# Turning every fourth tile of attention counts on TensorE instead of in a DMA transpose, with one DMA transpose per tile for the others

## The reference

```python
q = _fq_sym(q, axis=-1); k = _fq_sym(k, axis=-1); v = _fq_sym(v, axis=2)   # symmetric, 127 steps
attn = jnp.einsum('bhqd,bhkd->bhqk', q, k)
attn = softmax(attn)
attn = _fq_unsigned(attn, axis=-1)        # round(attn / (max/255)), 0..255
out = jnp.einsum('bhqk,bhkd->bhqd', attn, v)
```

## Time and profile before

| | |
|---|---|
| median of 3 runs | 1628.33 us |
| the profiled execution | 1632.03 us, its span 1630.3 us |
| PE, DVE, ACT, POOL busy | 84%, 62%, 46%, 26% of the span |
| mean granted clock of PE | 0.888 |
| first read of scores (L1816) to the end of the last | 1085.8 to 1452.5 us |

### The profile page before, as it was taken

One profiled execution on the slowest core, in us unless ns is written; L12 is line 12 of the kernel. 1 busy time (PEld: TensorE's weight loads), 2 busy tenths in 40 slices (PEclk: granted clock), 3 DMA queues, 4 the chain that ended last, 5 costly groups with the idle time before them and its releaser, 6 DMA issues.

```text
span 1630.3 us, 22435 instructions
## 1 busy us (share of the span) xinstructions
PE 1365.1 (84%) x7972; PEld 660.5 (41%) x7972; DVE 1017.6 (62%) x1722; ACT 756.4 (46%) x1094; POOL 428.8 (26%) x316
## 2 busy tenths in 40 slices
PE   7993989898857999999999999786677676659778
PEld 3441555555524444444444444322222222224334
DVE  5998899999965101111011110898889898864995
ACT  4774788888830111111111111327677776752553
POOL 1114100000004757999940002201111111100341
PEclk9996999999968999999999999877666766769989
DMA  7998565555348999999997996389999999993001
GB/s 252 290 278 165 106 130 117 131 115 115 63 155 304 356 373 368 368 402 395 408 359 294 316 367 225 81 186 212 208 213 212 206 210 210 205 186 78 1 1 52
DMA packets 516726, 355.12 MB, mean 218 GB/s; under 512 B 430856, under 2 KB 432904, under 8 KB 516016
## 3 DMA queue, kind: packets, MB, share of 16 engines
q1 hardware_dynamic: 502896, 308.08, 71.3%
q0 software_dynamic: 9920, 37.75, 6.6%
q10 hardware_dynamic: 3840, 8.39, 1.4%
HBM read 205.86 MB, written 38.01 MB: 150 GB/s over the span
## 4 chain that ended last, share of the span: by engine, by line
PE 48%; DMA 22%; DVE 17%; issue 8%; ACT 3%; POOL 1%; POOLq 0%; SPq 0%; ACTq 0%; DVEq 0%
DMA arena<-arena 20%; PE scores L1021 18%; PE bank L1039 9%; PE bank L904 4%; PE scores L887 2%; DVE arena L1601 2%; PE scores L888 2%; DVE arena L1587 2%; PE scores L1171 2%; ACT arena L1302 2%; PE bank L1207 1%; PE scores L1031 1%; PE scores L1092 1%; DVE arena L1816 1%; POOL arena L779 1%
## 5 line engine op out<-in xcount | busy, mean ns | idle before, releaser
L1816 DVE TENSOR_SCALAR_CACHE_REDUCE arena<-scores,arena 128x1024 f32<-128x1024 f32 x256 | 311.7, 1279 | 36.1 <-PE scores L1092 35.8
L1021 PE MATMUL scores<-arena 128*128 128x512 f32 x736 | 321.4, 595 | 3.3 <-DVE arena L1735 3.3
L1394 ACT ACTIVATE arena<-arena 128x2048 int16<-128x2048 f32 x128 | 255.8, 1999 | 129.2 <-DMA arena<-arena 98.0
L1743 DVE TENSOR_TENSOR arena<-scores,arena 128x512 f32<-128x512 f32 x46 | 31.8, 692 | 446.9 <-PE scores L1021 446.9
L1092 PE MATMUL scores<-arena 96*128 96x512 bf16 x512 | 205.9, 544 | 32.9 <-DVE arena L1816 27.9
L1021 PEld LDWEIGHTS scores<-arena 128*128 128x128 f32 x736 | 140.3, 191 | 180.2 <-issue 176.7
L1039 PE MATMUL bank<-arena 128*128 128x512 f32 x368 | 163.3, 597 | 3.6 <-issue 3.4
L1106 PE MATMUL bank<-arena 128*128 128x32 bf16 x2048 | 64.4, 183 | 94.0 <-DMA arena<-arena 93.9
L1587 DVE TENSOR_REDUCE arena<-scores 128x1 f32<-128x640 f32 (+3 forms) x128 | 127.8, 1019 | 8.5 <-PE scores L865 8.1
L1302 ACT ACTIVATE arena<-scores 128x512 f32<-128x512 f32 (+3 forms) x256 | 116.9, 507 | 25.9 <-PE scores L888 25.8
L1601 DVE TENSOR_TENSOR arena<-arena 128x1024 f16<-128x1024 f32 (+2 forms) x128 | 126.2, 1026 | 3.5 <-issue 1.8
(11 more groups left out here) (277 smaller groups left out, 2041.3 us busy)
## 6 DMA issues: line engine op xcount, KB each, us to landing
arena<-in_L_ffn_w SPq DMA_DIRECT2D x69, 2048.0 KB, 12.8
arena<-arena SPq DMA_DIRECT2D x32, 256.0 KB, 3.0
kst_d<-arena POOLq DMA_DIRECT2D x16, 384.0 KB, 6.6
tern_d<-arena POOLq DMA_DIRECT2D x12, 512.0 KB, 7.0
arena<-kst_d SPq DMA_DIRECT2D x16, 384.0 KB, 4.2
xs_d<-arena SPq DMA_DIRECT2D x23, 256.0 KB, 3.5
arena<-xs_d SPq DMA_DIRECT2D x22, 256.0 KB, 14.0
ys_d<-arena ACTq DMA_DIRECT2D x22, 256.0 KB, 6.7
```

The costliest lines, as they stand in the source:

```text
L1021: ins = pe.matmul(scores[:, m * 1024 + half * 512:m * 1024 + half * 512 + 512], xsT[a][:, c], wa[:, m, c, half * 512:half * 512 + 512], st ...
L1394: act.activation(p16[j % PAIRS_P][:, n % 2], ssb[n % SBUFS], ACT.Exp, bias=ebias[n % SBUFS], scale=-1.0, accum_out=rsum[h % 2][:, t:t + 1] ...
L1816: dve.tensor_scalar(ssb[i][:, d:d + 1024], scores[:, s:s + 1024], nsq[:, h, t:t + 1], None, ALU.mult, ALU.min, accum_out=nmx[i][:, half:ha ...
```

## The change

- `p16` and `pT` are used as 6 and 4 single tiles (`PBUFS`, `TBUFS`), in the same memory as the pairs.
- Three tiles of four (n % 4 = 0, 1, 2) are turned by a DMA transpose each, of 128 x 2048 counts (512 KiB). It waits for `av_done` of the tile four before.
- Tiles with n % 4 = 3 (`by_pe`) are turned on PE: the counts are taken as 1024 words of 32 bits, and 8 transposes of 128 x 128 words go into banks 4 and 5 (`a1_turn`, three tiles behind the scores). ACT copies both banks into `pT` (`copy_turned`, two copies of 128 x 512 words, behind the exponential of tile n + 2).
- A word holds two counts, so ACT writes the counts of such a tile in an interleaved order (four-dimensional patterns for `dst` and `src`), and the products read `pT` with a step of two elements between columns.
- Banks 4 and 5 are no longer free for scores: these go round two slots instead of three, half m in slot m % 2, and PE waits for the read of the half two before.
- The products stand five tiles behind the scores, one tile at a time, those of a turned tile six behind.
- Semaphores are shared to make room (`q0_in` with `x_loaded`, `wdT_in` with `wT_in`); what waits for them waits for correspondingly higher counts.

```diff
-PAIRS_P, PAIRS_T = 3, 2
+PBUFS, TBUFS = 6, 4
+        def by_pe(n):
+            return n % TBUFS == TBUFS - 1
...
-            for j in range(H * NT // 2):
-                i = j % PAIRS_T
-                if j >= PAIRS_T:
-                    sp.wait_ge(av_done, 2 * (j - PAIRS_T + 1))
-                sp.wait_ge(p_ready, 2 * j + 2)
-                sp.dma_start_transpose(pT[i].rearrange("p o c n -> p (o c) n"),
-                                       p16[j % PAIRS_P].rearrange("p o n -> p (o n)").bitcast(F16)).then_inc(pT_in[i], 16)
+            for n in range(H * NT):
+                h, t = divmod(n, NT)
+                if not by_pe(n):
+                    if n >= TBUFS:
+                        sp.wait_ge(av_done, n - TBUFS + 1)
+                    sp.wait_ge(p_ready, n + 1)
+                    sp.dma_start_transpose(pT_tile(n), p16_tile(n).bitcast(F16)).then_inc(pT_in[n % TBUFS], 16)
...
                 for m in (2 * n, 2 * n + 1):
-                    if m >= 3:
-                        pe.wait_ge(s_read, m - 2)
+                    if m >= 2:
+                        pe.wait_ge(s_read, m - 1)
...
+            def a1_turn(n):
+                pe.wait_ge(p_ready, n + 1)
+                words = p16_tile(n).bitcast(F32)
+                for g, bank in enumerate((bank4, bank5)):
+                    if n >= TBUFS:
+                        pe.wait_ge(pT_made, 2 * (n // TBUFS) - 1 + g)
+                    for c in range(4):
+                        ins = pe.transpose(bank[:, c * P:(c + 1) * P], words[:, (4 * g + c) * P:(4 * g + c + 1) * P], idf)
+                    ins.then_inc(p_turned, 1)
...
+                if by_pe(n):
+                    pe.wait_ge(pT_made, 2 * (n // TBUFS) + 2)
+                    pairs = pT_tile(n).rearrange("p c n -> p (c n)").rearrange("p (m q o) -> p m o q", m=NC // 2, o=2)
+                    tiles = [pairs[:, c // 2, c % 2] for c in range(NC)]
...
-            for n in range(H * NT):
-                a1_scores(n)
-                if n % 2 and n >= 7:
-                    a1_pv(n - 7)
+            for n in range(H * NT + 6):
+                if n < H * NT:
+                    a1_scores(n)
+                if 0 <= n - 3 < H * NT and by_pe(n - 3):
+                    a1_turn(n - 3)
+                if 0 <= n - 6 < H * NT and by_pe(n - 6):
                     a1_pv(n - 6)
-            for n in range(H * NT - 6, H * NT):
-                a1_pv(n)
+                if 0 <= n - 5 < H * NT and not by_pe(n - 5):
+                    a1_pv(n - 5)
...
+            def copy_turned(n):
+                for g, bank in enumerate((bank4, bank5)):
+                    act.wait_ge(p_turned, 2 * (n // TBUFS) + g + 1)
+                    if n >= TBUFS and g == 0:
+                        act.wait_ge(av_done, n - TBUFS + 1)
+                    act.activation(pT_words(n)[:, g * 512:(g + 1) * 512], bank.bitcast(I32), ACT.Copy).then_inc(pT_made, 1)
```

More of the change, by code:

```diff
@@ L199, in program @@
         consts_made = sem("consts_made")
-        x_loaded = [sem(f"x_loaded{j}") for j in range(2)]
+        x_loaded = q0_in = [sem(f"x_or_q0_in{j}") for j in range(2)]
+        X_IN = 16 * NT // 2
         wkv_loaded = sem("wkv_loaded")
@@ L438, in program @@
         p_ready = sem("p_ready")
-        pT_in = [sem(f"pT_in{i}") for i in range(PAIRS_T)]
+        pT_in = [sem(f"pT_in{i}") for i in range(TBUFS - 1)]
+        p_turned, pT_made = sem("p_turned"), sem("pT_made")
         av_done, a_post = sem("av_done"), sem("a_post")
@@ L1085, in a1_scores @@
                 if h == 0:
-                    pe.wait_ge(q0_in[t % 2], 16 * (t // 2 + 1))
+                    pe.wait_ge(q0_in[t % 2], X_IN + 16 * (t // 2 + 1))
                 for m in (2 * n, 2 * n + 1):
-                    if m >= 3:
-                        pe.wait_ge(s_read, m - 2)
+                    if m >= 2:
+                        pe.wait_ge(s_read, m - 1)
                     for j in range(2):
-                        s, k = (m % 3) * 1024 + j * 512, (m % 2) * 1024 + j * 512
-                        ins = pe.matmul(scores[:, s:s + 512], qhead[h % 2][0:K3, t * P:(t + 1) * P], khead[h % 2][0:K3, k:k + 512], start=True, stop=True)
+                        s = (m % 2) * 1024 + j * 512
+                        ins = pe.matmul(scores[:, s:s + 512], qhead[h % 2][0:K3, t * P:(t + 1) * P], khead[h % 2][0:K3, s:s + 512], start=True, stop=True)
                     ins.then_inc(s_done, 1)
+            def a1_turn(n):
[7 more added lines that the diff above has]
+                    ins.then_inc(p_turned, 1)
             def a1_pv(n):
                 h, t = divmod(n, NT)
-                j = n // 2
                 bank = (bank6, bank7)[h % 2]
-                if t % 2 == 0:
-                    pe.wait_ge(pT_in[j % PAIRS_T], 16 * (j // PAIRS_T + 1))
+                if by_pe(n):
+                    pe.wait_ge(pT_made, 2 * (n // TBUFS) + 2)
+                    pairs = pT_tile(n).rearrange("p c n -> p (c n)").rearrange("p (m q o) -> p m o q", m=NC // 2, o=2)
+                    tiles = [pairs[:, c // 2, c % 2] for c in range(NC)]
+                else:
+                    pe.wait_ge(pT_in[n % TBUFS], 16 * (n // TBUFS + 1))
+                    tiles = [pT_tile(n)[:, c] for c in range(NC)]
                 if t == 0:
@@ L1105, in a1_pv @@
                 for c in range(NC):
-                    ins = pe.matmul(bank[:, t * HD:(t + 1) * HD], pT[j % PAIRS_T][:, t % 2, c], vhead[h % 2][:, c], start=c == 0, stop=c == NC - 1)
+                    ins = pe.matmul(bank[:, t * HD:(t + 1) * HD], tiles[c], vhead[h % 2][:, c], start=c == 0, stop=c == NC - 1)
                 ins.then_inc(av_done, 1)
@@ L1196, in _ @@
                         turn_hidden(HIDDEN_TURNS.index(4 * t + q))
-            pe.wait_ge(wdT_in, 16)
+            pe.wait_ge(wT_in, 48)
             for t in range(NT):
@@ L1387, in exp_tile @@
                 h, t = divmod(n, NT)
-                j = n // 2
-                if n % 2 == 0 and j >= PAIRS_P:
-                    act.wait_ge(pT_in[(j - PAIRS_P) % PAIRS_T], 16 * ((j - PAIRS_P) // PAIRS_T + 1))
+                if n >= PBUFS:
+                    m = n - PBUFS
+                    if by_pe(m):
+                        act.wait_ge(p_turned, 2 * (m // TBUFS) + 2)
+                    else:
+                        act.wait_ge(pT_in[m % TBUFS], 16 * (m // TBUFS + 1))
                 if t == 0 and h >= 2:
@@ L1399, in _ @@
                 act.wait_ge(kT_in[a], 16 * (NC // 2 + NT // 2))
-            for n in range(H * NT):
-                exp_tile(n)
+            for n in range(H * NT + 2):
+                if n < H * NT:
+                    exp_tile(n)
+                if n >= 2 and by_pe(n - 2):
+                    copy_turned(n - 2)
             copy_rows(XT3, o_turned, oT_ready, (bank4, bank5))
```

33 lines of the change are left out of this document (21 added, 12 removed).

## The result

The changed kernel takes 1615.57 us (median of 4 runs, 1614.33 to 1617.59) against 1628.39 before: a ratio of 0.992 with an interval of 0.9908 to 0.9932. The forecast was 1618. The profiled execution took 1615.37 us, its span 1613.6 against 1630.3. The profiled execution of before lay 3.7 us above its median, so the spans differ by more (16.7) than the medians (12.8).

What follows compares the result with a forecast made beforehand. DVE's reads of scores were taken as the bound, with DMA making them wait. Reads -3 (330.9 + 30 + 3 = 364 against 366.7) and end -7 give -10: 1618 us from 1628.3; forecast 1611 to 1625, range 1600 to 1638.

Steps and rivals of the forecast that it cites:

- DMA is no longer the bound: SP's queue in the stage: six half-size transposes and loads take 17.6 us a head, under DVE's 20.7; 35.8 us stall goes.
- The half of 5.2 us for a single transpose: SP's queue: a 512 KiB transpose holds it for half of the 5.2 us that 1 MiB takes, near 2.6.
- PE's refills are late next: Two-slot score refills on PE: at low clock 2.08 us lost a round, most behind C; at high clock 0.2.
- The recurrence: One round of tiles D, A, B, C followed at low clock: 11.76 us against DVE's own 9.68.
- The size of the stall: DVE's waits for scores: 30 us, between 45 at low clock and 3 at full, with 36% at full clock.
- 3 at the start: First landings of the stage, sharing DMA with the loads of Wp as before: 3 us added to the reads.
- Transposes and the clock: A skill page says PE transposes don't count as busy, making stall 45 us; the prediction held that the trace contradicts it.
- The stationary operand with a step of two: Weight loads of turned tiles' products: cost taken as 0, with +95 us as the bound above.
- the value taken: ACT's interleaved exponential on turned tiles: unchanged duration, at most 10.0 us a round; +17 us if twice as long.
- The end: From the last exponential's start to the last products' end: 5.5 us instead of 12.2, so -6.7.
- The sum: Whole kernel: -3 from the reads and -7 from the end make -10, giving 1618 us.
- low clock all through: Rival: PE's refills behind C replace DMA's cost, 45 us of stall, +5 in all, 1633 to 1634 us; chance 18%.

Runs made afterwards that it cites:

- e2: The changed kernel with no tile turned on PE: all 128 by DMA transposes of 512 KiB, scores in three slots again; 1640.19 us, ratio 1.0059.
- e7: The changed kernel with the loads of Wp and bp moved to the end of the third head, POOL's additions of bp later too; 1613.42 us, ratio 0.9902.
- e3: The changed kernel with only two of the eight PE transposes of a turned tile, copies and products as before; 1613.13 us, ratio 0.9892.
- e4: The changed kernel with the exponential of turned tiles written in plain order instead of interleaved; 1616.98 us, ratio 0.9915.
- e5: The changed kernel with the third score slot given back, PE transposes in two lumps of four, finish_head one tile earlier; 1594.61 us, ratio 0.9789.

## Why the prediction was right

**DMA is no longer the bound: right.** Landings in 4.4 us, the queue with gaps, 6.1 us of waits for landings in the weight loads of products. e2 shows that it is the share moved to PE, and not the smaller transposes, that did it. The half of 5.2 us for a single transpose held roughly: full of singles, DMA moved 204 GB/s against 209. Products wait more than half a microsecond for a landing only in the first head, see below.

**PE's refills are late next: right, but the place only in part.** DVE's loss before a read, worked out as the distance of two reads' starts less 1.21 us (less 1.34 more where `finish_head` lies between), from the second head on, by the clock half a microsecond before the read:

| tile, first half | low clock: times, sum, mean | full clock: times, sum, mean |
|---|---|---|
| A (n % 4 = 0) | none | 30, 0.0, 0.00 |
| B (n % 4 = 1) | 11, 1.4 us, 0.13 | 19, 0.0, 0.00 |
| C (n % 4 = 2) | 30, 13.8 us, 0.46 | none |
| D (n % 4 = 3) | 3, 2.9 us, 0.98 | 27, 7.4 us, 0.27 |

Second halves lose nothing. The recurrence had 0.09, 0.50 and 1.4 for B, C and D at low clock. C is met (0.46) and B nearly. But the prediction said that most is lost behind C, so at D, with one wait there. It is the other way round: C, whose refill stands behind two tiles' products, is late in all 30 rounds and loses more than half, 13.8 of 25.5 us, and D loses 10.3. `finish_head` hides the loss at D in every other round, as forecast. In the other fifteen rounds the clock of the transposes themselves decides: in nine all eight started at low clock, and D lost 0.9 to 1.4 us; in six at least five of the eight started at full clock, and D lost 0.4 us at most.

The windows of one round show how D comes to be at full clock nearly always (PE busy, clock, DMA share, GB/s):

```profile
1201.40:1204.80 3.40, 3.40 (x19) 0.50 0.74 120
1204.80:1208.20 3.40, 2.32 (x39) 0.99 1.00 203
1208.30:1211.70 3.40, 2.13 (x25) 0.99 1.05 196
1211.70:1215.10 3.40, 3.28 (x30) 0.50 0.12 25
```

Here PE works through the lump behind C without a gap at low clock, and the clock rises at its end, just before D. Then, with PE idle for a third of the time, it falls again for the next B and C. So the two levels are not spread at random over the tiles: in each of the 31 rounds it rises within 2 us of the eight transposes.

**The size of the stall: met, in part by luck.** Forecast were 30 us of stall and 3 at the start on top of 330.9. Measured are 361.2 - 330.9 = 30.3. By the distances of reads it is 25.5 us in the table and 6.4 in the first head (together 1.6 more; the two ways of counting differ by that). Of the first head's, waits of 3.84 and 1.64 us stand at tiles 6 and 7, where the products five tiles behind met landings held up by Wp; with these loads moved the first head is 3.0 us shorter (e7). So the steady stall was forecast too high, as the clock was full for 52% of the time (a mean of 0.76) and not for 36%, and the start too low: 3 was kept "as before", though the products now stand five tiles behind and not six or seven. The two errors were small and of opposite sign. DVE's waits by the profile, 25.2 us, lie at the very edge of the 25 to 38 forecast. That a mean share of the clock decides the stall was too simple, as e3 shows from the other side: less work, a lower clock, and only 4.7 us less.

**Transposes and the clock.** The reading weighed in the prediction, that transposes do not count as busy PE (the Trainium skill, TensorE: Matmul & The Clock Gate, Part 4: PE-mode transpose), is not borne out here: the stretch 1201.4 to 1204.8 contains all eight of a lump, and 0.99 follows; with six of eight left out the stage's clock falls from 0.76 to 0.61. By that page's rule leaving them out would not lower the clock.

**The stationary operand with a step of two: right at 0.** All products' weight loads in the changed kernel have a mean of 102 ns, a quarter of the 2048 with the step:

```profile
L1134 PEld LDWEIGHTS bank<-arena 128*128 128x128 f16 x2048 | 70.3, 102 | 28.9 <-issue 13.8 <-DMA arena<-arena 6.1
```

The Trainium skill (same page, Weight-path perf modes) had it that a step of this size keeps the fast load, and the trace agrees, 102 ns against 101 before. At low clock the products of turned tiles stand 0.030 us apart and those of the others 0.027, some 0.04 us a tile and 1 us in all; whether the step or their place behind the transposes causes it was not tried. At full clock both stand 0.025 apart (three turned tiles).

**ACT: the value taken was wrong, without effect.** An interleaved exponential takes 2.5 us, not 2.0 (e4), which the prediction had named as a sign of being wrong. It was said that ACT has room for more than that, and so it was.

**The end: -6.7 forecast, -6.2 measured,** short by the 0.5 us of the slower exponential. **The sum:** -10 forecast, -12.8 by the medians. The reads gave 5.5 us where 3 were forecast. Behind the stage the span is 2.0 us shorter, where the prediction had said that nothing changes; the full clock at the start of the projection stands beside this and was not tried as its cause.

Of the rivals, low clock all through was nearest in mechanism: PE did take DMA's place and gave back most of what DMA had cost (30 of 36 us). It stayed on the faster side as half the time was at full clock. And the place that this rival names, behind C, holds only 10.3 of the 25.5 us.

## What to carry to other kernels

When a resource is freed, the buffers that it had made worthless become the bound: the third slot gained nothing while DMA was full, and the kernel that has it back beside PE's turning, with the transposes in two halves, is 21 us faster. Lay added work in pieces no longer than the gap that the engine has between two refills, as the same transposes in pieces of two and three, with no third slot, gained 18 us. Two tiles' products in a row cost more here than the eight transposes, whose cost was the one looked for. And take what a change will cost from the place in the round where it falls, not from an engine's share of busy time.

## What was not expected of the hardware

- **PE's clock depends on how the same work is bunched.** With the same matmuls the stage's mean clock was 0.68 with three slots and DMA as the bound, 0.54 with two. In the changed kernel's order it was 0.76, and 0.81 with the pieces spread, where the stage is also 19 us shorter.
- **A DVE instruction is slower with POOL's copy beside it.** `finish_head`'s last step takes 0.72 us where POOL's copy of values runs at the same time, 14 times of 16 in the kernel before and in the changed one, and 0.42 in the two heads where it doesn't. In the changed kernel and in e5, where `finish_head` comes one tile before that copy (min/median/max ns):

```profile
L1873 DVE TENSOR_TENSOR arena<-arena x16: 424/724/728, 1127.8 to 1451.2; 128x256 f32<-128x256 f32 x16
```

```profile
L1880 DVE TENSOR_TENSOR arena<-arena x16: 424/425/426, 1122.8 to 1426.7; 128x256 f32<-128x256 f32 x16
```

  It is worth 0.3 us a head, some 4.2 us of e5's gain. That the copy is the cause was not tried by itself.
- **An exponential that writes in steps of two elements and reads in four dimensions costs a quarter more,** 2.53 against 2.00 us for 128 x 2048. Which of the two patterns costs it was not tried.
- **First reads of the stage start anywhere in 4.5 us** (1081.6 to 1086.1) in kernels whose code up to there is the same or differs only in semaphore numbers. A difference of spans between two single profiles is no finer than that.
